# A k-nearest-neighbour graph convolution on one core: embeddings and features moved to idle PSUM banks, a gather reordered by pieces, and flags put ahead of scatters

## The reference

```
emb  = x_flat @ dist_w.T                  # 1024 x 32
d2   = |e_n|^2 + |e_m|^2 - 2 e_n.e_m
adj  = (m among the 24 nearest of n) and (dist <= 10), or n == m
X    = x_flat @ fc_w.T + fc_b             # the "features"
S    = (adj / De) @ adj.T / Dv            # Dv: row sums, De: column sums
out  = S @ X + x_flat
o    = batchnorm(out over 4 images), then o * sigmoid(o)
result = x + o
```

## Time and profile before

| | us |
|---|---|
| median of 3 runs | 205.23 (205.18 to 209.13) |
| the profiled execution's own time | 205.92 |
| its span, first to last instruction | 203.8 |
| PE busy | 177.9 |
| DVE busy | 156.1 |
| ACT busy | 118.9 |
| POOL busy | 85.2 |

### The profile page before, as it was taken

How to read it: one execution, slowest core, us unless ns; L and a number is a source line. 1 busy time by engine, 2 the same in 40 slices (tenths; PEclk the granted TensorE clock), 3 DMA queues, 4 the chain that set the end, 5 groups by cost and what they waited for, 6 DMA issues and landing times.

```text
span 203.8 us, 4396 instructions
## 1 busy us (share of the span) xinstructions
PE 177.9 (87%) x1338; PEld 100.7 (49%) x1338; DVE 156.1 (77%) x912; ACT 118.9 (58%) x207; POOL 85.2 (42%) x120
## 2 busy tenths in 40 slices
PE   7999988889999959999899969999986999999400
PEld 2336352236547636545366645555564577757300
DVE  1789959779998549985995098999999873695664
ACT  2157779687687869637656697444485322060192
POOL 1004821469424169932060689845226751320000
PEclk9999999579999996999999999999999999999955
DMA  5801000155327426422293642442442199610038
GB/s 168 305 5 1 2 3 0 9 99 101 58 54 89 64 6 128 84 53 51 52 60 49 53 106 53 82 77 51 53 56 51 10 125 223 85 30 0 0 115 298
DMA packets 44404, 14.83 MB, mean 73 GB/s; under 512 B 41813, under 2 KB 42453, under 8 KB 44378
## 3 DMA queue, kind: packets, MB, share of 16 engines
q1 hardware_dynamic: 43514, 14.14, 39.4%
q10 hardware_dynamic: 864, 0.40, 0.7%
HBM read 4.02 MB, written 2.13 MB: 30 GB/s over the span
## 4 chain that ended last, share of the span: by engine, by line
PE 36%; DVE 24%; issue 13%; DMA 8%; POOL 8%; ACT 7%; DVEq 2%; SPq 1%; ACTq 0%; POOLq 0%
DVE cand L790 9%; PE pg L366 8%; PE pt L391 7%; PE po L410 6%; PE pt L410 5%; DMA inv_rows<-rdv 5%; POOL H L697 4%; PE pt L431 4%; DVE top L805 3%; DVE cwork L810 3%; DMA dvb<-inv_rows 3%; DVEq L829 2%; DVE xn L992 2%; DVE prod L904 2%; PE pg L343 1%
## 5 line engine op out<-in xcount | busy, mean ns | idle before, releaser
L790 DVE MAX8 cand<-key 128x8 f32<-128x64 f32 x512 | 81.2, 210 | 2.0 <-ACT key L568 1.2
L391 PEld LDWEIGHTS pt<-xp,H 128*128 128x128 bf16 x768 | 45.7, 99 | 22.1 <-issue 14.9
L391 PE MATMUL pt<-xp,H 128*128 128x128 bf16 (+1 forms) x768 | 50.6, 223 | 2.4 <-issue 2.0
L568 ACT ACTIVATE key<-pg 128x512 f32<-128x512 f32 x64 | 35.0, 593 | 26.0 <-PE pg L366 26.0
L366 PE MATMUL pg<-right,left 64*128 64x512 f32 x128 | 47.3, 675 | 3.0 <-ACT key L568 1.4
L576 ACT ACTIVATE sign<-key,thr 128x1024 bf16<-128x1024 f32 x32 | 36.7, 1146 | 11.9 <-DVE thr L816 11.9
L692 POOL TENSOR_SCALAR low<-cs 128x1 f32<-128x1 f32 x32 | 6.0, 187 | 69.7 <-ACT sign L576 66.9
L410 PE MATMUL po<-HT,tp 128*128 128x512 bf16 x144 | 34.0, 380 | 1.1 <-ACT tp L589 0.7
L697 POOL TENSOR_SCALAR H<-sign 128x1024 bf16<-128x1024 bf16 x32 | 33.4, 1043 | 2.5
L366 PEld LDWEIGHTS pg<-right,left 64*128 64x128 f32 x128 | 14.0, 192 | 17.6 <-issue 8.8
L410 PEld LDWEIGHTS po<-HT,tp 128*128 128x128 bf16 x144 | 12.7, 98 | 15.1 <-ACT tp L589 1.2
(11 more groups left out here) (91 smaller groups left out, 199.2 us busy)
## 6 DMA issues: line engine op xcount, KB each, us to landing
out<-xn SPq DMA_DIRECT2D x7, 256.0 KB, 2.1
dvb<-inv_rows SPq DMA_DIRECT2D x3, 512.0 KB, 5.7
x_sb<-x SPq DMA_DIRECT2D x1, 1024.0 KB, 6.2
x_sb<-x SPq DMA_DIRECT2D x1, 512.0 KB, 3.7
HT<-H SPq DMA_TRANSPOSE x32, 3.2
x_sb<-x ACTq DMA_DIRECT2D x1, 256.0 KB, 3.2
x_sb<-x SPq DMA_DIRECT2D x1, 256.0 KB, 3.6
out<-xn SPq DMA_DIRECT2D x2, 128.0 KB, 2.5
```

Source lines behind the costliest of these rows:

```text
L391: mm = pe.matmul(pt[:, j // T_BLOCKS, at:at + wide], lhs, x_cols(b, t, q, wide), start=(t == 0 and j % T_BLOCKS == 0 and q == 0), stop=(t ...
L568: act.activation(key[:, k % KEYS, cols], pg[:, h, :], ACT.Copy).then_inc(s["drained"], 1)
L790: ins = dve.max(cand[:, k % 2, c, :], key[:, k % KEYS, c * CHUNK:(c + 1) * CHUNK])
```

## The change

Seven edits, all of order and place; the arithmetic stays.

1. The embeddings of images 1 to 3 and the features of images 0 to 2 go through `po`, in an order of their own (`po_pair`, semaphores `po_filled` and `po_drained`). The features of image 3 stay in `pg`.
2. Their steps are new. Embeddings of images 1, 2, 3: k = 0, 5, 10 (before 1, 6, 14). Features of image 1: half 0 at k = 3, half 1 at 4 (before both at 1); image 2: k = 8 and 9 (before 9); image 3: both at 18 (before 17). `drain_x`, `operands` and the pieces are by halves, `norms` stands one step behind `embed`, and the middle piece of X is made by POOL instead of ACT.
3. `gather` goes by pieces: high piece for both halves, then middle, then low (image 3 as before). So the first half is ready after 40 of 48 products, not after 24. The last steps take 12, 14, 14, 8 products instead of 12, 14, 12, 10.
4. `out_part` of image b-2 stands at steps t = 1 and t = 2 (before at t = 7 of the image before and at t = 4); `y_stats` of images 0 and 1 move behind the loop.
5. On PE `flag(k-1)` stands ahead of the scatter; in steps 8b+3 the scatter stands ahead of both `fill_key` and `flag`.
6. At the start: `group_stats(2, 3)` moves behind the writing of the operands, `group_stats(3, 4)` behind the first candidates; the first candidates wait for half a key; fewer fillers (5 less), group means and inverse for images 2 and 3 later.
7. SP's `norms_out` and `norms_in`, POOL's `normalise(2)` and `(3)` and `residual` are moved to fit.

```diff
+EMB_STEPS = {0: 1, 5: 2, 10: 3}
+X_STEPS = {3: [(1, 0)], 4: [(1, 1)], 8: [(2, 0)], 9: [(2, 1)], 18: [(3, 0), (3, 1)]}
...
+        po_pair = {("emb", 0): 0, ("x", 0): 1, ("emb", 1): 2, ("x", 1): 3, ("emb", 2): 4, ("x", 2): 5, ("emb", 3): 6}
...
-                GATHER[b, t] = (b - 1, (12, 14, 12, 10)[t - T_STEP] if b == B - 1 else 8)
+                GATHER[b, t] = (b - 1, (12, 14, 14, 8)[t - T_STEP] if b == B - 1 else 8)
...
+            def gather_order(b):
+                n = len(parts(b))
+                if b == B - 1:
+                    return [(part, q) for part in range(n) for q in range(PIECES)]
+                return [(part, q) for q in range(PIECES) for part in range(n)]
...
+                    if q == 0 and j == 0 and b == 0:
+                        pe.wait_ge(s["po_drained"], 2 * po_pair["emb", B - 1] + part + 1)
...
+                    settled = RELEASE[k - 1] if k > 0 else []
+                    if b > 0 and t == LAG:
+                        for kk in settled:
+                            scatter(kk)
+                    if k + AHEAD < ALL:
+                        fill_key((k + AHEAD) // TILES, (k + AHEAD) % TILES)
                     if k > 0:
                         flag(k - 1)
+                    if not (b > 0 and t == LAG):
+                        for kk in settled:
+                            scatter(kk)
+                    if k in EMB_STEPS:
+                        embed(EMB_STEPS[k])
+                    if k - 1 in EMB_STEPS:
+                        norms(EMB_STEPS[k - 1])
+                    for bb, h in X_STEPS.get(k, []):
+                        fill_x(bb, h)
+                    if k == 1:
+                        group_variances(2, 2, B)
                     if (b, t) in GATHER:
                         gather(*GATHER[b, t])
...
                     if k > 0:
                         mark(k - 1)
-                    if k == 1:
+                    if k == 2:
                         group_sd(2, 2, B)
+                    if k - 2 in EMB_STEPS:
+                        operands(EMB_STEPS[k - 2], 1)
...
+                    if k + AHEAD < ALL:
+                        drain_key((k + AHEAD) // TILES, (k + AHEAD) % TILES)
+                    if k in EMB_STEPS:
+                        squares(EMB_STEPS[k])
+                    if k - 1 in EMB_STEPS:
+                        operands(EMB_STEPS[k - 1], 0)
+                    for bb, h in X_STEPS.get(k, []):
+                        drain_x(bb, h)
...
+            def x_pieces(b, h):
+                pool.wait_ge(s["x_hi"], 4 * b + 2 * h + 2)
+                pool.tensor_tensor(x_tiles(xr32, h), x_tiles(x32, h), x_piece(b, h, 0), ALU.subtract)\
+                    .then_inc(s["x_res"], 1)
+                pool.wait_ge(s["x_res"], 2 * b + h + 1)
+                pool.tensor_copy(x_piece(b, h, 1), x_tiles(xr32, h)).then_inc(s["x_mid"], 1)
+                pool.wait_ge(s["x_mid"], 2 * b + h + 1)
+                pool.tensor_tensor(x_piece(b, h, 2), x_tiles(xr32, h), x_piece(b, h, 1), ALU.subtract)\
+                    .then_inc(s["x_lo"], 1)
...
+                    for i, (bb, h) in enumerate(X_STEPS.get(k - 1, [])):
+                        if i == 0:
+                            x_pieces(bb, h)
+                    if b == B - 2 and t == TILES - 1:
+                        x_pieces(B - 1, 1)
...
             group_scale(1, 1, 2)
+            dve.wait_ge(s["x_in23"], 16)
+            group_stats(2, 3)
+            group_inverse(1, 1, 2)
+            candidates(0, range(CHUNKS))
             dve.wait_ge(s["step"], group_stats(3, B))
             group_moments(2, B)
-            candidates(0, range(CHUNKS))
-            group_inverse(1, 1, 2)
...
-                    if k == 1:
+                    if k == 2:
                         group_inverse(2, 2, B)
                     for kk in RELEASE[k]:
                         release(kk)
+                    if b > 1 and t == 1:
+                        out_part(b - 2, 0)
+                    if b > 1 and t == 2:
+                        out_part(b - 2, 1)
...
-                    if b > 0 and t == TILES - 1:
-                        out_part(b - 1, 0)
-                    if b > 1 and t == T_STEP:
-                        out_part(b - 2, 1)
-                    if b > 1 and t == TILES - 1:
-                        y_stats(b - 2, 0)
-                        y_stats(b - 2, 1)
+
+            out_part(B - 2, 0)
+            for h in range(2):
+                y_stats(0, h)
+            y_stats(1, 0)
```

More of the change, by code:

```diff
@@ L182, in build @@
         g_sums = [misc, misc, pt[:, 0, :]]
-        def emb_bank(b, h):
-            return (pg if b > 0 else po)[:, h, :]
         block = ctx.enter_context(nc.Block())
-        first_pairs = [("key", 0, 0), ("key", 0, 1), ("x", 0, 0), ("key", 0, 2), ("key", 0, 3)]
+        first_pairs = [("key", 0, t) for t in range(AHEAD)]
         def pairs_of_step(b, t):
@@ L284, in _ @@
                         inverse_in(b - 1)
-                    if t == TILES - LAG and b + 2 < B:
-                        norms_out(b + 2)
-                    if t == TILES - LAG + 1 and b + 2 < B:
-                        norms_in(b + 2)
+                    for step, image in EMB_STEPS.items():
+                        if image > 1 and b * TILES + t == step + 2 - LAG:
+                            norms_out(image)
+                        if image > 1 and b * TILES + t == step + 3 - LAG:
+                            norms_in(image)
                     if t == TILES - 1 and b < B - 1:
@@ L524, in first_operands_end @@
                 copy_left(0, slice(0, P), HALF, N).then_inc(s["l0_made"], 1)
-            def operands(b):
-                for h, cols in halves():
-                    act.wait_ge(s["n_filled"], 2 * b + h + 1)
-                    if b > 1:
-                        act.wait_ge(s["norm_out"], 16 * b)
-                    copy_left(b, slice(0, P), h * HALF, (h + 1) * HALF).then_inc(s["l_made"], 1)
-                    act.activation(right[:, b % 2, cols], emb_bank(b, h), ACT.Identity, scale=cst[:, C_LR + 2:C_LR + 3],
-                                   bias=cst[:, C_LR + 3:C_LR + 4]).then_inc(s["r_made"], 1)
-                for h in range(2):
-                    act.wait_ge(s["l_made"], 2 * (b - 1) + h + 1)
-                    act.wait_ge(s["r_made"], 2 * b + h + 1)
-                    act.sem_inc(s["drained"], 1)
@@ L554, in x_middle @@
[L554 to L559 removed]
+                for h in range(2):
+                    act.wait_ge(s["l0_made"], 2 + h)
+                    act.sem_inc(s["po_drained"], 1)
@@ new lines, in operands @@
+            def operands(b, h):
+                cols = slice(h * HALF, (h + 1) * HALF)
+                act.wait_ge(s["n_filled"], 2 * b + h + 1)
+                if b > 1:
+                    act.wait_ge(s["norm_out"], 16 * b)
+                copy_left(b, slice(0, P), h * HALF, (h + 1) * HALF).then_inc(s["l_made"], 1)
+                act.activation(right[:, b % 2, cols], po[:, h, :], ACT.Identity, scale=cst[:, C_LR + 2:C_LR + 3],
+                               bias=cst[:, C_LR + 3:C_LR + 4]).then_inc(s["r_made"], 1)
+                act.wait_ge(s["l_made"], 2 * (b - 1) + h + 1)
+                act.wait_ge(s["r_made"], 2 * b + h + 1)
+                act.sem_inc(s["po_drained"], 1)
@@ new lines, in drain_x @@
+            def drain_x(b, h):
+                cols = slice(h * HALF, (h + 1) * HALF)
+                if ("x", b) in po_pair:
+                    act.wait_ge(s["po_filled"], 2 * po_pair["x", b] + h + 1)
+                else:
+                    act.wait_ge(s["filled"], 2 * pair["x", b, 0] + h + 1)
+                if b > 0:
+                    act.wait_ge(s["x_lo"], 2 * (b - 1) + h + 1)
+                if b >= XBUFS:
+                    act.wait_ge(s["h_used"], TILES * (b - XBUFS + 1))
+                act.activation(x32[:, cols], x_bank(b, h), ACT.Copy).then_inc(s["x_hi"], 1)
+                act.wait_ge(s["x_hi"], 4 * b + 2 * h + 1)
+                act.sem_inc(s["po_drained" if ("x", b) in po_pair else "drained"], 1)
+                act.activation(x_cols(b, slice(h * TH, (h + 1) * TH), 0),
+                               x32[:, cols].rearrange("p (t c) -> p t c", c=C), ACT.Copy).then_inc(s["x_hi"], 1)
@@ L602, in _ @@
             first_operands_end()
-            drain_x(0)
             drain_key(0, 2)
-            x_middle(0)
+            for h in range(2):
+                drain_x(0, h)
             drain_key(0, 3)
@@ L787, in candidates @@
                 if 0 in chunks:
-                    dve.wait_ge(s["drained"], 2 * pair["key", k // TILES, k % TILES] + 2)
+                    dve.wait_ge(s["drained"], 2 * pair["key", k // TILES, k % TILES] + (1 if k == 0 else 2))
                 for c in chunks:
+                    if k == 0 and c == CHUNKS // 2:
+                        dve.wait_ge(s["drained"], 2 * pair["key", 0, 0] + 2)
```

(1 more changed line is left out.)

145 lines of the change are left out of this document (39 added, 106 removed).

## The result

The changed kernel takes 212.38 us in the median (211.12 to 213.9, 4 runs) against 207.18 for the kernel before (205.18 to 209.48, 4 runs); the ratio is 1.034, with an interval of 1.024 to 1.043. It is slower. I had forecast 205.4 and no measurable change; the time lies just inside my wide range (197 to 213), outside the likeliest one (202 to 209), on the side of rival B.

What follows compares the result with a forecast made beforehand. PE (34.3 us an image) and DVE (33.8) were taken as balanced, with order costing on top; 1.0 later at S(28) less 0.8 in the tail gave span 204.0, time 205.4; likeliest range 202 to 209, wide 197 to 213.

Steps and rivals of the forecast that it cites:

- rival B: Slower: PE gaps in steps 5 to 12 bring the 1.2 GHz clock, +6 to 9 us, 211 to 214; chance 0.28.
- The signs: PE waiting for `low` in most image 0 steps; DVE's longest wait at `scale_t(0)`; about 38 us between its first ends.
- The start: Edit 6, DVE's new order: the first `limit` 1.3 us later, part of it hidden by a shorter root wait.
- S(0): Start of DVE's `limit` in step 0: 18.10 us before, forecast 19.4.
- S(3): Start of DVE's `limit` in step 3: forecast 32.4 us, with a root wait of about 1.3.
- the ring: Image 0: PE's scatter waits for flag, `low`, ACT's mark and drain of PE's last extra item; 32.8 us against 22.9.
- S(12): Start of DVE's `limit` in step 12, an end of `scale_t`: 75.95 us before, forecast 79.5.
- Images 1 and 2: Steps 12 to 28: first piece forecast 37.9 us, where it was 42.6; second 37.3, before 35.1.
- The tail: From step 28 to the end: gather by pieces and earlier flag(30) save 0.8 us; uncovered `y_stats` cost at most 1.9.
- Rival A: Faster: ACT reaches each mark in time, the flag ring does not bind; S(12) = 67.8, 193 to 196 us; chance 0.27.
- S(28): Start of DVE's `limit` in step 28, an end of `scale_t`: 153.73 us before, forecast 154.7.
- S(8): Start of DVE's `limit` in step 8: forecast 50.9 us, as nothing starves DVE of keys.

Runs made afterwards that it cites:

- e6: The e1 kernel with DVE's old order at the start, both statistics blocks where they stood before: 199.09 us, ratio 0.962.
- e1: The changed kernel with PE's flag moved back behind the scatter and the embedding or features of its step: 195.79 us, ratio 0.945.
- e2: The changed kernel with the flag behind the scatter but still ahead of the embedding or features: 204.8 us, ratio 0.985.
- e9: The changed kernel with PE's order untouched; on ACT, squares, first half of operands and drain_x stand one step later, behind the mark: 197.7 us, ratio 0.959.
- e3: The kernel before with one edit, the flag ahead of the scatter: 212.78 us, ratio 1.027.
- e4: The changed kernel with small unread products on PE ahead of the flag in steps 5 to 10, 12 and 20: 209.8 us, ratio 1.013.
- e7: The e1 kernel with the key ahead of the scatter in steps 11, 19 and 27: 200.52 us, ratio 0.972.
- e10: The e1 kernel with gather, out_part, y_stats, start and key-scatter order as in the kernel before: 197.55 us, ratio 0.957.
- e11: The best follow-up kernel (194.68 us) with five unread 512-column products in PE's steps 1 to 3, instead of three or none: 198.47 us, ratio 0.958.

## Why the prediction was right and wrong

- **What bounds the kernel.** Right: the three ends of `scale_t` are the points where the time is made, and the pieces between them moved with the signs forecast.
- **The signs.** Those for the forecast came: PE waits for `low` 14 times, DVE's longest wait is 10.8 us at `scale_t(0)`, and 39.6 us lie between the first two ends for "about 38". The sign for rival B did not: from 30 to 80 us the granted clock is 0.93, and in the kernel before it was 0.91. A mean over image 0 could not show where the low clock did its harm, on the items that PE had just been kept waiting for.
- **The start.** S(0) came at 19.54 for 19.4. S(3) = 32.99, 0.6 late, as DVE waited 2.96 us for the root where I had 1.3. e6, with DVE's old order, has the early S(0) and is no earlier at S(3) (32.59), so the 1.3 us that I booked for this order was not its loss; which other part of the change puts S(3) behind the 31.56 of the kernel before is open.
- **Image 0, the ring.** Right in its links and in its size per turn, 5.46 for 5.6; e1, e2 and e9 show it from three sides, and e3 brings the same waits into the old kernel. S(12) was 2.4 us later than forecast. 1.3 of them are there when the second half of features 1 ends, at 44.5 for 43.2, of which 1.0 is the low clock on the first half (2.07 for 1.11). The rest comes in the ring, 34.0 us for 32.8, although scatter(6) (2.07 for 1.56) and embedding 3 (3.13 for 1.93) alone took 1.7 more at the low clock; its other turns were 0.5 shorter than priced.
- **Images 1 and 2.** Right that 42.6 shrinks and 35.1 grows. The sizes were off by 1.7 and 1.3 us; scatter(8), the gather behind it and scatter(16) ran at the low clock, 2.76 us for 1.56 each scatter. With that clock held up in e4 both pieces are within 0.8 us of the forecast (37.1 and 37.1 for 37.9 and 37.3).
- **The tail.** The forecast gain of 0.8 was 0.2. The moved `y_stats` are covered here, as I had said: DVE waits 1.00 us for flag(31) behind them, and the two last scatters run without a gap. What was not in the sum is scatter(24) at the low clock behind the wait for flag(27), 2.77 us for 1.56. Only in the e1 kernel, where PE is earlier, do the `y_stats` hold `read_flag(31)`, and the last scatter waits 1.1 us for its release.
- **Rival A** did not happen in the change, but its sum was close to what the kernel does without the ring: it gave S(12) = 67.8 and 193 to 196 us; e1 has 69.7 and 195.8. That is closer than the sum deserves, as it had no term for the clock, and in e7, also without the ring, a low clock puts S(12) at 77.0.
- **Rival B** happened in part. The step that failed is the sum of the ring: I priced its turns, and the steps 12 and 20 behind it, at the upper clock, and put the clock's share only into a rival, although the gaps of 2 us that stand ahead of it were a part of the forecast itself. By the rows the low clock lengthened items of PE by 1.0 (features 1) + 1.7 + 1.2 (scatter(8)) + 1.7 (eight gather products in 3.60 us for 1.89) + 1.2 (scatter(16)) + 1.2 (scatter(24)) = 8.0 us; the span was missed by 6.0. The waits absorb some of it, and e4, which holds up only a part of these stretches, gives back 2.6 to 4. So that the clock made the miss is shown for the pieces from S(12) to S(28) by e4; for image 0 and the tail it is read from the rows alone. Why the clock falls behind some of these gaps and not behind others stays open. The remaining 1.0 us to the time is the step from profile to median, for which I had taken off 0.7: the median of the changed kernel lies 0.4 above its profiled execution.
- **Two rules of the Trainium skill.** The Trainium skill ("Perfetto Trace Analysis", Matmuls) says that independent groups should rotate through different PSUM banks, so that draining one overlaps the next. e10 is in line with it, 4.3%, but banks, halves and steps moved together there, so no run here prices the banks by themselves. The Trainium skill ("TensorE: Matmul & The Clock Gate", A second HAM failure mode) describes short idle times between groups that make the clock swing. The five stretches at 0.50 in the changed kernel, with 19.4 us of waits for `low`, and none until 183 us in e1, with 3.9, agree with it.

## What to carry to other kernels

Ahead of moving a small step earlier on an in-order engine, follow what it waits for back through the other engines' orders: if one of them reaches it only after serving this engine's own last item, the move closes a ring, and where its turn is longer than each engine's work it becomes the step time, here 5.46 us for 3.8 of PE's own. Such a ring can be opened at either end, here by placing the flag behind the items (16.6 us) or the mark ahead of the drains (14.7 us). A forecast with repeated gaps on PE should carry what follows them at the lower clock as a term of its sum, since it cost 1.0 to 2.9 us at each place here. And a bundle of edits that measures slower can hide a part that is worth 4%.

## What the runs showed of the hardware

- The clock falls in some executions of one and the same kernel and not in others: e1 took 195.6 to 195.9 us three times, with a mean clock of 0.973, and 199.9 once with 0.951. PE's rows from 22 to 34 us are the same to 0.01 us, but for a shift of 0.38, in e1 and in the profiled execution of e6: PE had waited 1.46 us for a `low` in both, and the key behind it took 1.61 us in one and 2.56 in the other, where the clock fell at 34.6 and rose at 41.6. So these rows do not decide whether it falls.

```profile
34.19 1.61 PE L375 MATMUL pg<-right,left 64*128 64x512 f32 x4 [0.42 <-ACT key L581]
...
34.57 2.56 PE L375 MATMUL pg<-right,left 64*128 64x512 f32 x4 [0.42 <-ACT key L581]
```

- More unread products ahead of such a place do not keep the clock up for certain (e11): in its profiled execution the clock fell 20 us later.
- What such a fall costs depends on who is late: in e7 DVE reaches S(8) in time (51.31, 50.86 in e1) with the clock down from 34.6 to 41.5 us, and with the second stretch, 58.5 to 62 us, some 6 us come out at S(12), where DVE needs PE's last scatter.
